# A two-layer graph network on one core: aggregation and expert product alternate graph by graph, and routing is done for two graphs at a time

## The reference

```python
h = jnp.maximum(_layernorm(x, axis=-1), 0.0)
x = x + _L0_gnn_ref(h, adj, adj, Wq, Wk, Wv, Wo)      # attention, 16 heads, biased by 2 * adj
h = jnp.maximum(_layernorm(x, axis=-1), 0.0)
x = x + _L1_gnn_ref(h, adj, router_w, router_b, expert_w, bn_gamma, bn_beta)
...
scores = x.mean(axis=1) @ router_w + router_b         # one row of 4 scores for a graph
top1 = jnp.argmax(scores, axis=-1)                    # the graph's expert
W = expert_w[top1]                                    # 512x512
out = adj @ (x @ W)
# batch norm with mean and variance over all graphs of one expert, then relu
```

## Time and profile before

| | before |
|---|---|
| time, median of 3 runs | 1625.91 us (1625.65 to 1627.64) |
| the profiled execution, its span | 1624.5 us |
| PE busy | 1414.4 us, 87% of the span |
| DVE busy | 1220.7 us, 75% |
| ACT busy | 931.5 us, 57% |
| POOL busy | 539.8 us, 33% |
| expert stage, first Z on PE to last P | about 1152 to 1453 us from the span's start |
| final stage, without PE | 1472 to 1624 us |

### The profile page before, as it was taken

One profiled execution on the slowest core, in us unless ns is written; L12 is line 12 of the kernel. 1 busy time (PEld: TensorE's weight loads), 2 busy tenths in 40 slices (PEclk: granted clock), 3 DMA queues, 4 the chain that ended last, 5 costly groups with the idle time before them and its releaser, 6 DMA issues. The chain is left out here.

```text
span 1624.5 us, 38099 instructions
## 1 busy us (share of the span) xinstructions
PE 1414.4 (87%) x10994; PEld 1211.5 (75%) x10995; DVE 1220.7 (75%) x2645; ACT 931.5 (57%) x2957; POOL 539.8 (33%) x593
## 2 busy tenths in 40 slices
PE   7999999999999999999999999998799999982000
PEld 6888888888888888888888888886577777772000
DVE  4777777777777777777777777776676667758998
ACT  4677676676766766766766766766455454520000
POOL 0222222223232232222232232222234344425655
PEclk9999999999999999999999999998799999996555
DMA  5955566655666545666555666545243322127963
GB/s 185 249 135 123 135 150 155 151 126 119 147 154 154 142 119 128 150 156 147 137 119 139 151 155 149 123 108 143 92 144 129 129 96 80 46 72 269 342 228 124
DMA packets 144864, 235.52 MB, mean 145 GB/s; under 512 B 17842, under 2 KB 34226, under 8 KB 144818
## 3 DMA queue, kind: packets, MB, share of 16 engines
q1 hardware_dynamic: 136370, 218.20, 51.7%
q10 hardware_dynamic: 8448, 16.78, 2.8%
HBM read 92.30 MB, written 41.94 MB: 83 GB/s over the span
## 5 line engine op out<-in xcount | busy, mean ns | idle before, releaser
L268 POOL TENSOR_TENSOR prob<-prob,norm 128x512 f32<-128x512 f32 x256 | 266.7, 1042 | 789.2 <-DVE norm L372 789.2
L301 ACT ACTIVATE prob<-logits,neg_max 128x128 f32<-128x128 f32 x1024 | 398.1, 394 | 70.0 <-DVE neg_max L361 69.9
L43 PE MATMUL bank<-hT_hi,w_hi 128*128 128x256 f32 x1024 | 303.6, 296 | 2.8 <-DVE hT_lo L405 2.5
L43 PE MATMUL bank<-hT_lo,w_hi 128*128 128x256 f32 x1024 | 291.3, 284 | 0.0
L43 PE MATMUL bank<-hT_hi,w_lo 128*128 128x256 f32 x1024 | 291.1, 284 | 0.0
L356 DVE SCALAR_TENSOR_TENSOR logits<-scores_ps,adj 128x512 f32<-128x512 f32 x256 | 176.7, 690 | 133.6 <-PE scores_ps L420 132.7
L308 ACT ACTIVATE probT<-probT_ps 128x512 f32<-128x512 f32 x256 | 152.7, 596 | 143.0 <-PE probT_ps L427 143.0
L43 PEld LDWEIGHTS bank<-hT_hi,w_hi 128*128 128x128 f32 x1024 | 197.2, 193 | 21.4 <-issue 19.2
L43 PEld LDWEIGHTS bank<-hT_lo,w_hi 128*128 128x128 f32 x1024 | 197.8, 193 | 0.0
L43 PEld LDWEIGHTS bank<-hT_hi,w_lo 128*128 128x128 f32 x1024 | 197.4, 193 | 0.0
L301 ACT ACTIVATION_READ_ACCUMULATOR prob<-logits,neg_max 128x1 f32 x1024 | 195.5, 191 | 0.0
(11 more groups left out here) (127 smaller groups left out, 2875.2 us busy)
## 6 DMA issues: line engine op xcount, KB each, us to landing
stack<-qk SPq DMA_DIRECT2D x768, 128.0 KB, 2.5
x_in<-in_x SPq DMA_DIRECT2D x32, 512.0 KB, 4.7
x_res<-in_x SPq DMA_DIRECT2D x64, 256.0 KB, 2.8
x_dram<-x_res SPq DMA_DIRECT2D x64, 256.0 KB, 2.8
x_in<-x_dram SPq DMA_DIRECT2D x32, 512.0 KB, 3.7
y<-outs ACTq DMA_DIRECT2D x16, 1024.0 KB, 5.2
out_dram<-outs SPq DMA_DIRECT2D x32, 256.0 KB, 2.0
w_hi<-x_dram SPq DMA_DIRECT2D x8, 1024.0 KB, 9.6
```

The costliest lines, as they stand in the source:

```text
L43: last = nc.tensor.matmul(out, a, b, start=(n == 0), stop=(n == len(terms) - 1))
L268: nc.gpsimd.tensor_tensor(prob[:, slot], prob[:, slot], norm[:, slot].unsqueeze(2).to_broadcast([N, R, N]), ALU.mult).then_inc(normed, 1)
L301: last = nc.scalar.activation(prob[:, slot, r], logits[:, slot, r], ACT.Exp, bias=neg_max[:, slot, r:r + 1], accum_out=row_sum[:, slot, r: ...
```

## The change

In the expert stage PE no longer does two Z in a row and two P in a row: each P of the old group is followed by a Z of the new one. M is done twice for each group, for graphs 0 and 1 and for graphs 2 and 3. M0 stands in the iteration of its own group, M1 one iteration later (`AHEAD` gives M1 -1), and P0 of an iteration needs M0, P2 needs M1. The two graphs of an M lie on two partitions: `mean_h` is laid out so that one matmul takes two graphs as stationary columns, and `top1` has two rows. DVE's M has five instructions where it had six: compare and multiply are one scalar_tensor_tensor. The counts for the batch norm are summed over the two partitions by the matmul that spread them before, and their maximum and reciprocal are taken after it, on 128 partitions. ACT's A, DVE's N and S3, and SP's loads get new places.

```diff
-    mean_h = sb("mean_h", [128, G, KC])
+    mean_h = sb("mean_h", [128, KC, G])
...
-    top1 = sb("top1", [1, B], I32)
+    top1 = sb("top1", [2, B // 2], I32)
...
-    PE_ORDER = "Z0 Z1 J P0 P1 Z2 P2 Z3 P3 M"
-    ACT_ORDER = "A2' A3' Z0 P0 A0 A1 Z1 P1 Z2 P2 Z3 P3"
-    DVE_ORDER = "M' Y0 Y1 S3' N0 Z0 S0 Z1 S1 Y2 N1 Z2 S2 Y3 J Z3"
-    POOL_ORDER = "N0 P0 N1 P1 P2 P3"
-    SP_ORDER = "X1 P0 X0 P1 J P2 P3"
...
+    PE_ORDER = "P0 M1 Z0 P1 Z1 P2 M0 Z2 P3 J Z3"
+    ACT_ORDER = "P0 A2 Z0 P1 A3 Z1 P2 A0 Z2 P3 A1 Z3"
+    DVE_ORDER = "M1 Y0 Z0 S0 Y1 N0 Z1 S1 M0 Y2 Z2 S2 Y3 J Z3 S3 N1"
+    POOL_ORDER = "P0 P1 N0 P2 P3 N1"
+    SP_ORDER = "P0 P1 X1 P2 P3 X0 J"
+    AHEAD = {"sp": {"X0": 2, "X1": 1, "J": 2, "P": -1}, "pe": {"J": 1, "P": -1, "M1": -1},
+             "act": {"A0": 1, "A1": 1, "P": -1}, "dve": {"N": 1, "J": 1, "S": -1, "M1": -1}, "pool": {"N": 1, "P": -1}}
...
+    START = {("act", -1): "A0 A1 U2", ("act", 0): "A2 Z0 A3 Z1 U3 A0 Z2 A1 Z3",
+             ("dve", -1): "N0 N1 J U2", ("dve", 0): "Y0 Z0 Y1 N0 Z1 M0 Y2 Z2 U3 Y3 J Z3 N1"}
+
+    def expert_of(group, g):
+
+        return top1[g % 2:g % 2 + 1, bass.ds(2 * group + g // 2, 1)]
...
-                        nc.vector.tensor_tensor(best[:], score[:], score_max[:].unsqueeze(2).to_broadcast([1, G, E]),
-                                                ALU.is_ge).then_inc(router_step, 1)
-                        wait(dve, router_step, 4 * group + 3)
-                        nc.vector.tensor_tensor(candidate[:], best[:], expert_less_e[:].unsqueeze(1).to_broadcast([1, G, E]),
-                                                ALU.mult).then_inc(router_step, 1)
...
+                        nc.vector.scalar_tensor_tensor(out=candidate[:], in0=score[:], scalar=score_max[:], in1=expert_less_e[:],
+                                                       op0=ALU.is_ge, op1=ALU.mult).then_inc(router_step, 1)
...
-            then_wait(nc.vector.tensor_copy(inv_count[:], router_ps[:, 0:E]))
+            then_wait(nc.vector.tensor_scalar(all_count[:], router_ps[:, 0:E], float(N), 1.0, ALU.mult, ALU.max))
+            then_wait(nc.vector.reciprocal(inv_count[:], all_count[:]))
...
-                        for k in range(G):
-                            for c in range(KC):
-                                last = nc.tensor.matmul(router_ps[0:1, E * k:E * k + E], mean_h[:, k, c:c + 1], rw[:, c],
-                                                        start=(c == 0), stop=(c == KC - 1))
+                        for c in range(KC):
+                            last = nc.tensor.matmul(router_ps[0:2, 0:E], mean_h[:, c, 2 * g:2 * g + 2], rw[:, c],
+                                                    start=(c == 0), stop=(c == KC - 1))
...
-                        if g == 0:
-                            wait(pe, routed, group + 1)
-                        e = pe.value_load(top1[0:1, bass.ds(n, 1)], min_val=0, max_val=E - 1)
+                        if g % 2 == 0:
+                            wait(pe, routed, 2 * group + g // 2 + 1)
+                        e = pe.value_load(expert_of(group, g), min_val=0, max_val=E - 1)
```

More of the change, by code:

```diff
@@ L507, in expert_layer @@
     z_lo = sb("z_lo", [128, G, KC, N], F32R)
-    mean_h = sb("mean_h", [128, G, KC])
+    mean_h = sb("mean_h", [128, KC, G])
     sums = sb("sums", [N, 2, E, D])
     rw = sb("rw", [128, KC, E])
[L511 to L517, removed]
-    top1 = sb("top1", [1, B], I32)
+    rb = sb("rb", [2, E])
+    expert_less_e = sb("expert_less_e", [2, E])
+    score = sb("score", [2, E])
+    score_max = sb("score_max", [2, 1])
+    candidate = sb("candidate", [2, E])
+    first = sb("first", [2, 1])
+    top1 = sb("top1", [2, B // 2], I32)
     bn = sb("bn2", [N, G, 6])
@@ L715, in body @@
                         n = G * group + g
-                        if g == 0:
-                            wait(pool, routed, group + 1)
-                        e = pool.value_load(top1[0:1, bass.ds(n, 1)], min_val=0, max_val=E - 1)
+                        if g % 2 == 0:
+                            wait(pool, routed, 2 * group + g // 2 + 1)
+                        e = pool.value_load(expert_of(group, g), min_val=0, max_val=E - 1)
                         wait(pool, out_copied, n + 1)
@@ L790, in count_rows @@
             def count_rows():
-                dve.wait_ge(routed, GROUPS)
+                dve.wait_ge(routed, 2 * GROUPS)
                 for e in range(E):
@@ L826, in body @@
                         if g == 0 and isinstance(group, int):
-                            dve.wait_ge(routed, group + 1)
-                        e = dve.value_load(top1[0:1, bass.ds(n, 1)], min_val=0, max_val=E - 1)
+                            dve.wait_ge(routed, 2 * group + 2)
+                        e = dve.value_load(expert_of(group, g), min_val=0, max_val=E - 1)
                         wait(dve, squared, n + 1)
@@ L848, in body @@
                     elif token == "M":
-                        if isinstance(group, int) and group == 0:
+                        r = 2 * group + g
+                        if isinstance(r, int) and r == 0:
                             dve.wait_ge(consts, 2)
-                            dve.wait_ge(const_loaded, 64)
-                        wait(dve, router_scored, group + 1)
-                        nc.vector.tensor_tensor(score[:], router_ps[0:1, 0:G * E].rearrange("p (g e) -> p g e", g=G),
-                                                rb[:].unsqueeze(1).to_broadcast([1, G, E]), ALU.add).then_inc(router_step, 1)
@@ L861, in body @@
-                        nc.vector.tensor_tensor(candidate[:], best[:], expert_less_e[:].unsqueeze(1).to_broadcast([1, G, E]),
-                                                ALU.mult).then_inc(router_step, 1)
-                        wait(dve, router_step, 4 * group + 4)
+                            dve.wait_ge(const_loaded, 80)
+                        wait(dve, router_scored, r + 1)
+                        nc.vector.tensor_tensor(score[:], router_ps[0:2, 0:E], rb[:], ALU.add).then_inc(router_step, 1)
@@ L864, in body @@
                         nc.vector.tensor_reduce(first[:], candidate[:], X, ALU.min).then_inc(first_ready, 1)
-                        wait(dve, first_ready, group + 1)
-                        nc.vector.tensor_scalar(top1[:, bass.ds(G * group, G)], first[:], float(E), float(E - 1), ALU.add,
+                        wait(dve, first_ready, r + 1)
+                        nc.vector.tensor_scalar(top1[:, bass.ds(r, 1)], first[:], float(E), float(E - 1), ALU.add,
                                                 ALU.min).then_inc(routed, 1)
@@ L970, in _ @@
             pe.wait_ge(count_ready, 1)
-            nc.tensor.matmul(router_ps[:, 0:E], ones[0:1, :], inv_count1[:], start=True, stop=True).then_inc(inv_count_made, 1)
+            nc.tensor.matmul(router_ps[:, 0:E], ones[0:2, :], count[:], start=True, stop=True).then_inc(inv_count_made, 1)
             for n in range(2 * E):
```

44 lines of the change are left out of this document (20 added, 24 removed).

## The result

The changed kernel takes 1608.46 us (median of 4 runs, 1606.58 to 1609.86) where the kernel before took 1626.78 (4 runs, 1625.65 to 1628.62). The ratio is 0.9885 with an interval of 0.9871 to 0.9899: faster by 1.15%. The forecast was 1600, with 1590 to 1614 as the range. So the sign and the range held, but over a quarter of the forecast gain of 25.6 us did not come, and the time lies outside the 1595 to 1605 of the forecast itself, in the part of the range that was there for the rival with DVE as the bound.

What follows compares the result with a forecast made beforehand. PE (15.9 to 16.3 us) and DVE (15.9) bound together; with 0.6 for the port, 16.5 an iteration. Fifteen save 21.1 us, start 3.5, end 1.2, less 0.2: 25.6 less, 1600 us, range 1590 to 1614.

Steps and rivals of the forecast that it cites:

- the rival with DVE as the bound: Expert stage: chain over N1, POOL, A2, Z0 and port waits bind DVE; 17.3 us an iteration, 1612 us; chance 0.20.
- Routing off the path: Expert stage: M0 and M1 have 5.2 and 4.6 us of cover against DVE's 2.4 to 3.5, if DVE is in time.
- PE's floor: PE's work per expert iteration, 15.8 to 16.3 us, lower bound 15.9; as a rival 1591 us, chance 0.25.
- DVE's loop: DVE's expert iteration: 13.6 us of instructions plus built-in waits, N1 loop and loop's edge, 15.9 us.
- the loop's edge: DVE at the iteration's end: a branch no longer behind a long instruction, some 0.2 us.
- The time on the port: DVE meeting POOL in the expert stage: up to 2.1 us by chance hits, mostly absorbed, 0.6 us an iteration taken.
- a rival of 18.7 us: Expert stage: DVE and POOL fall in step, lengthening top, candidate and S; 18.7 us an iteration, 1633 us; chance 0.06.
- The prediction's sign of being wrong: Expert stage: the forecast would be wrong if DVE shows fewer waits and intervals above 17 us.
- What meets POOL: DVE in the expert stage: two top, two candidate and four S an iteration may be hit, 0.27 us each.
- the rule's case: DVE's candidate held up by POOL: 0.27 us more twice an iteration, 8 us over 15, time near 1608.
- Start: First P0 of the expert stage: comes sooner as J, N1 and Z3 move later; 3.5 us less.
- End: Last four P of the expert stage follow Z3 at once instead of waiting for routing; 1.2 us less.

Runs made afterwards that it cites:

- small sum: Changed kernel with POOL adding only 16 of the 512 columns to `sums`, the rest of the means left out; 1593.72 us, ratio to before 0.9797.
- the two with more on DVE: Kernel with POOL's sum on 16 columns, plus one or two extra 128x512 subtractions on DVE ahead of Z2; 1594.68 and 1601.87 us.

## Why the prediction was right, and which term was too small

**Routing off the path: right.** P0 waits for routing once in the steady iterations, for 0.17 us at 1317.21, behind a candidate that POOL held up. **PE's floor: right**, forecast as 15.8 to 16.3 with a lower bound of 15.9, and 16.13 as measured. Four P at 2.97 or 2.88, four Z at 0.81 to 0.92, J 0.44 and two M at 0.27 make it up; issue behind M did not come.

**DVE's loop: nearly right**, 15.9 worked out against 16.1 measured. One piece was larger than taken: the loop's edge has 0.35 us of issue ahead of score, not 0.2. And the 0.36 ahead of each S was put down to the read of `top1` from a row in which the wait is for ACT's square; in the changed kernel it stands as issue ahead of S2 (0.23), and as a wait for square elsewhere (0.32 ahead of the S0 at 1259.41). The price held; which of the two sets it was not tried.

**The time on the port: the mis-sized term.** The prediction took 0.6 us an iteration on top of 15.9, as chance hits of eight instructions of which most is absorbed by waits. A steady iteration takes 16.95, which is DVE's 16.1 and 0.85. Not only the size but the picture behind it was wrong. The hits are not spread: one S per iteration meets one sum of POOL, at the same place each time, and loses 0.84 to 1.05. No built-in wait stands behind it that could take it up, since J, Z3, S3, N1 and M1 follow without a wait for z_hi. The prediction had such a lock only as a rival of 18.7 us, with top and candidate in it. Of the 0.45 us that a steady iteration takes more than 16.5, some 0.25 are from this term and 0.2 from DVE's loop. What happened lies between the forecast and the rival in which DVE becomes the bound (17.3 an interval, 1612 us), and is of that rival's kind: PE waits, once in most iterations (P2 in 11 of 14), for a DVE that has no slack. The prediction's sign of being wrong, fewer waits on DVE and intervals above 17, is half there: DVE's waits for z_hi did become fewer (24.5 us against 35.3), all 15 intervals take 17.01 in the mean, and those behind 1317 take 17.0 to 17.3 but for the last two. That the time lies in the range is in part luck: the lock on which the time hangs was meant to be left out of it, and was priced too high.

**What meets POOL: partly wrong.** top was counted among those that may be hit, from its 157 to 1173 ns. In the kernel before it starts inside a POOL sum in 14 of 16 cases and takes 0.90 to 1.17 us in all of these; in the changed kernel it takes 141 to 144 ns in all 32 cases, the 11 inside a sum among them. So it is the new form of top that is not held up, and not its new place. Which part of the form counts, one column instead of four or two partitions instead of one, was not tried. For candidate the prediction weighed L372 with its 166 ns at most against a rule of the Trainium skill ("SBUF — State Buffer", "Who interferes with whom"). With 1281 ns at the longest, and 1.13 to 1.28 in nine iterations in a row of the kernel with N1 ahead of P3, candidate does wait for POOL. By that rule, a DVE instruction with two SBUF inputs is held up by a GpSimd instruction that reads SBUF and began first; the trace agrees for S and candidate. It was 4 hits in 32 though, and not two an iteration. That the 1608 of the rule's case is the time measured is luck: its 8 us came from another line, S2.

**Start: right**, 3.3 us against 3.5. The first interval's excess is 1.2 us against 1.7 (18.11 against 16.95): P0 takes 5.02 at first, after a wait of 4.38, but the first interval has no long S.

**End: wrong sign.** Forecast were 1.2 us less for the last four P; measured 0.3 more. They do run at full clock, 1.00 against 0.87. But M1 of the last group came behind an S of 1.81 us. DVE of the changed kernel there, and PE:

```profile
1423.01 1.81 DVE L836 TENSOR_TENSOR sums<-sums,square 128x512 f32 x1
...
1425.53 0.14 DVE L867 TENSOR_SCALAR top<-first 2x1 int32<-2x1 f32 x1
```

```profile
1426.56 0.49 PE L43 MATMUL out_ps<-w_hi,z_hi 128*128 x1 [1.08 <-DVE top L867]
```

P2 waited 1.08 us. With z_hi first on ACT, nothing waits there, and the last four P take 11.90 us, the 1.1 us less that the forecast meant. **Not foreseen** were the 1.3 us in the transposes of `sums`, at a lower granted clock (0.55 against 0.70).

**In sum**, the forecast gain was 25.6 us. The intervals gave 5.9 less than forecast, the start 0.2 less, the end 1.5 less, the transposes 1.3 less and the final stage and batch norm 0.2 less, while 1.9 came from the attention stage: 25.6 - 9.1 + 1.9 = 18.4.

## What to carry to other kernels

When a change takes a wait off one engine's path, work out the loop of each engine, and where two come within a few tenths of a microsecond, the slack is nil and any lengthened instruction is the iteration's; where one has time to spare, as DVE without its S, the same meeting costs nothing. Read the min, median and max of each short line and look whether the long ones stand at the same place in every iteration: that is a meeting, not noise, and it is not to be averaged. Try then to shift one order list by one place on each engine in turn; such one-line edits made this kernel some 8 us worse (0.9934 against 0.9885 of the time before) or 15.8 us better, and which one does what could only be measured.

## What the runs showed of the hardware

- A meeting of DVE and POOL repeats to a tenth of a microsecond over iterations and executions: S2 at 1266.65 and 1266.71, 1.55 us both. All 4 long candidates and the long S of the changed kernel come again in its second execution. Small shifts decide it: with S2 0.29 us behind the start of POOL's sum it takes 1.55, with S2 0.40 ahead 0.69.
- What is held up beside a POOL sum, and what is not: S (128x512, 0.69 us alone and up to 1.83 over all kernels), candidate (2x4, 0.21 and up to 1.32), top as 1x4 (0.16 and up to 1.17), m<-bn (128x2, 0.15 and up to 1.26). Not held up when they start inside a sum: top as 2x1 (11 cases in the changed kernel, 0.14) and z_lo, whose input z_ps is in PSUM (15 cases, 0.69).
- POOL is held up by DVE as well: beside S1 of DVE shift takes 0.65 us where it takes 0.20 alone, and the sum that starts beside S0 takes 1.55 where others take 1.28. POOL of the changed kernel:

```profile
1259.71 1.55 POOL L728 TENSOR_TENSOR sums<-sums,outs 128x512 f32 x1 [0.25 <-POOL sums L728]
...
1263.31 0.65 POOL L716 TENSOR_TENSOR shift<-neg_mean,rstd 128x2 f32<-128x2 f32 x1
```

- The granted clock over the 36 instructions of the transposes of `sums` was 1.00 in three of the variants (z_hi first, S2 before Z2, small sum), 0.70 in three (both sums on POOL, and the two with more on DVE) as in the kernel before, and 0.54 or 0.55 in the changed kernel, in that with N1 ahead of P3 and in that with M split in the old order. In the changed kernel and that with N1 ahead of P3 P2 of the last group had waited 1.08 us; in the third of these it had waited 0.24. What decides stays open, as nothing was tried on it.
